# A PDE stage's first slots: four chunks' second parts and the images times 0.3 made ahead of them

## The reference

```
ux, uy = Sobel_x(u), Sobel_y(u)          uxx, uxy, uyy = Sobel of these    (all clipped to +-10)
g2 = ux*ux + uy*uy
K  = clip((uxx*uyy - uxy*uxy) / ((1+g2)^2 + eps), -5, 5)
H  = clip(((1+uy*uy)*uxx - 2*ux*uy*uxy + (1+ux*ux)*uyy) / (2*sqrt(1+g2+eps)^3 + eps), -5, 5)
u  = u + 0.01 * clip(alpha*K + beta*H, -1, 1);   border pixels := their inner neighbours
ten times; result = 0.7*u + 0.3*x
```

## Time and profile before

| | us |
|---|---|
| median of 3 runs | 767.97 (766.85 to 768.89) |
| the profiled execution's own time | 767.58 |
| its span in the profile | 765.8 |
| busy PE / DVE / ACT / POOL | 666.3 / 437.4 / 371.2 / 324.5 |
| curvature stage, from its first stencil product | 424.03 to the end |

### The profile page before, as it was taken

How to read it: one execution, slowest core, us unless ns; L and a number is a source line. 1 busy time by engine, 2 the same in 40 slices (tenths; PEclk the granted TensorE clock), 3 DMA queues, 4 the chain that set the end, 5 groups by cost and what they waited for, 6 DMA issues and landing times.

```text
span 765.8 us, 11096 instructions
## 1 busy us (share of the span) xinstructions
PE 666.3 (87%) x4344; PEld 462.5 (60%) x4344; DVE 437.4 (57%) x642; ACT 371.2 (48%) x620; POOL 324.5 (42%) x311
## 2 busy tenths in 40 slices
PE   5997898999975556688998879999999999999994
PEld 4773774565442223444464768777777878777782
DVE  5630000095041012222434469999999999999997
ACT  1310000060000001110223469999999999999995
POOL 1000000010032400000001469999999999999993
PEclk9999999999995779999999979999999999999997
DMA  9999999999999999999962000000000000000001
GB/s 340 432 406 403 407 419 413 428 421 409 424 401 391 419 427 424 431 427 423 426 274 93 1 0 1 0 0 0 0 0 0 0 0 0 0 0 0 0 0 55
DMA packets 20945, 166.52 MB, mean 217 GB/s; under 512 B 1840, under 2 KB 2224, under 8 KB 11568
## 3 DMA queue, kind: packets, MB, share of 16 engines
q1 hardware_dynamic: 19552, 162.60, 51.5%
q0 software_dynamic: 688, 2.04, 0.8%
q10 hardware_dynamic: 672, 1.41, 0.5%
HBM read 164.99 MB, written 1.05 MB: 217 GB/s over the span
## 4 chain that ended last, share of the span: by engine, by line
DVE 33%; DMA 28%; PE 25%; issue 7%; ACT 4%; POOL 2%; DVEq 0%; POOLq 0%; SPq 0%; ACTq 0%
DMA ring<-wout_w 15%; PE bank L373 6%; DVE ring L863 6%; PE bank L389 5%; DVE ring L868 5%; DVE ring L850 4%; PE bank L523 4%; PE bank L442 4%; PE bank L497 4%; DMA ring<-wv_p 4%; DVE bank L847 3%; DVE bank L883 3%; DMA ring<-wv_w 3%; DMA ring<-wqk_p 3%; DMA ring<-wout_p 3%
## 5 line engine op out<-in xcount | busy, mean ns | idle before, releaser
L574 PE MATMUL bank<-u_parts,vmr 128*128 128x480 f32 x1360 | 313.4, 388 | 13.2 <-DVE ring L863 6.3
L574 PEld LDWEIGHTS bank<-u_parts,vmr 128*128 128x128 f32 x1360 | 253.1, 190 | 73.7 <-DVE reg_a L857 15.4
L389 PE MATMUL bank<-ring,small 128*32 128x256 f32 x1152 | 79.5, 424 | 36.2 <-DMA ring<-wout_w 32.3
L389 PEld LDWEIGHTS bank<-ring,small 128*32 128x32 f32 x1152 | 39.3, 119 | 69.6 <-issue 30.3
L389 PE MATMUL bank<-ring,xw 128*32 128x256 f32 x1024 | 63.9, 410 | 15.8 <-DMA ring<-wv_w 15.8
L1086 POOL MEMSET reg_d<- 128x2176 f32 x1 | 1.9, 1916 | 151.8 <-PE bank L449 151.8
L1114 POOL DMA_DIRECT2D vmr<-vmats x1 | 0.6, 566 | 148.0 <-PE bank L389 148.0
L702 DVE SCALAR_TENSOR_TENSOR reg_a<-bank,prm 128x512 f32<-128x512 f32 x4 | 2.8, 692 | 105.7 <-PE bank L449 105.7
L373 PE MATMUL bank<-reg_a,ring 128*128 128x256 f32 x256 | 57.9, 388 | 3.4 <-DMA ring<-wqk_p 2.6
L389 PEld LDWEIGHTS bank<-ring,xw 128*32 128x32 f32 x1024 | 34.0, 117 | 44.0 <-DMA ring<-wv_w 19.5
L994 ACT ACTIVATE reg_e<-xa 32x384 f32<-32x384 f32 (+7 forms) x20 | 9.1, 457 | 98.3 <-DVE xa L831 72.1
(11 more groups left out here) (195 smaller groups left out, 1008.0 us busy)
## 6 DMA issues: line engine op xcount, KB each, us to landing
ring<-wv_w SPq DMA_DIRECT2D x32, 2048.0 KB, 24.0
ring<-wout_w SPq DMA_DIRECT2D x30, 2048.0 KB, 36.7
ring<-wqk_p SPq DMA_DIRECT2D x4, 2048.0 KB, 20.1
ring<-wqk_w SPq DMA_DIRECT2D x4, 2048.0 KB, 21.9
ring<-wv_p SPq DMA_DIRECT2D x2, 2048.0 KB, 22.9
ring<-wout_p SPq DMA_DIRECT2D x2, 2048.0 KB, 22.5
ring<-wout_w SPq DMA_DIRECT2D x4, 1024.0 KB, 36.0
vmr<-vmats POOLq DMA_DIRECT2D x1, 1664.0 KB, 7.2
```

Of the source, the lines that this page charges most:

```text
L389: ins = te.matmul(bank[32 * j:32 * j + 32, b_, n0:n0 + 256], lhs(c), slot[k % NSLOT][:, c, 256 * j:256 * j + 256], start=start and c == 0, ...
L574: last = te.matmul(dst[:, 0:NF], mat(m, first), p3[:, 2 + off:S + off, :], start=(high and n == 0), stop=(not high and n == len(terms) - 1))
```

## The change

ACT makes the SECOND parts of all four chunks' `u_hi`, then all four `x3`, before its slot 1; POOL makes the SECOND parts of all four `u_lo` before its slot 1. Slots 1 and 2 hold no `high` and no `low` any more, slots 1 to 4 no `x3`. The instructions are the same in kind, number and size; PE's, DVE's and SP's lists are the same as before.

```diff
 ACT
-            def slot_step(k, q, new, old, c, first=False):
+            def slot_step(k, q, new, old, c):
...
                 if c is not None:
-                    high(k + 2, c, not first or k + 2 > NCH)
+                    high(k + 2, c, True)
...
                 a.activation(fields_in(q, 0, 2), den[q].rearrange("p (x n) -> p x n", x=2), ACT.Exp,
                              scale=-1.0).then_inc(ac["inv"], 1)
-                if first and k <= NCH:
-                    a.activation(x3[:, k - 1, :], u_in(k - 1), ACT.Copy, scale=0.3).then_inc(ac["x3"], 1)
...
-            for x in range(2):
+            for x in range(NCH):
                 high(x + 1, x, False)
+            for x in range(NCH):
+                a.activation(x3[:, x, :], u_in(x), ACT.Copy, scale=0.3).then_inc(ac["x3"], 1)
             a.wait_ge(ve["scales"], 1)
             for k in range(1, LOOP_FROM):
-                slot_step(k, k % 2, True, k > 1, (k + 1) % NCH, True)
+                slot_step(k, k % 2, True, k > 1, (k + 1) % NCH if k + 2 > NCH else None)
 POOL
-            def slot_step(k, q, c, new, old, later=True, border=None):
+            def slot_step(k, q, c, new, old, border=None):
...
                 if c is not None:
-                    low(k + 1 if later else k + 2, c, later)
+                    low(k + 1, c)
...
-            for x in range(2):
+            for x in range(NCH):
                 low(x + 1, x, False)
             for k in range(1, LOOP_FROM):
                 if k + 2 <= NCH:
-                    slot_step(k, k % 2, k + 1, True, k > 1, False)
+                    slot_step(k, k % 2, None, True, k > 1)
                 else:
-                    slot_step(k, k % 2, k % NCH if k >= NCH else None, True, True, True, (k - 3) % NCH)
+                    slot_step(k, k % 2, k % NCH if k >= NCH else None, True, True, (k - 3) % NCH)
```

More of the change, by code:

```diff
@@ L1158, in _ @@
                 if k + 2 <= NCH:
-                    slot_step(k, k % 2, k + 1, True, k > 1, False)
+                    slot_step(k, k % 2, None, True, k > 1)
                 else:
-                    slot_step(k, k % 2, k % NCH if k >= NCH else None, True, True, True, (k - 3) % NCH)
+                    slot_step(k, k % 2, k % NCH if k >= NCH else None, True, True, (k - 3) % NCH)
             with p.Fori(1, LOOPS + 1) as i:
                 for m in range(NCH):
-                    slot_step(i * NCH + (m + 3), (m + 3) % 2, (m + 3) % NCH, True, True, True, m % NCH)
+                    slot_step(i * NCH + (m + 3), (m + 3) % 2, (m + 3) % NCH, True, True, m % NCH)
             for k in range(LOOP_END, SLOTS + 2):
-                slot_step(k, k % 2, k % NCH if k < SLOTS else None, k <= SLOTS, True, True, (k - 3) % NCH if k + 2 <= SLOTS else None)
+                slot_step(k, k % 2, k % NCH if k < SLOTS else None, k <= SLOTS, True, (k - 3) % NCH if k + 2 <= SLOTS else None)
     return nc
```

## The result

The changed kernel takes 758.07 us (median of 4 runs, 757.21 to 759.15) against 768.43 for the kernel before (four runs; the 767.97 given ahead is the median of the first three): ratio 0.9869, 95% interval 0.9848 to 0.9889, so 10.4 us faster. The forecast was 757.5, range 755.9 to 761.0. The profiled execution has a span of 756.5 us (765.8 before).

The account below looks back on a forecast made before the run. The prediction took the bound to be one wait handed from ACT's late high through POOL and DVE to PE in slots 1 and 2. Gains of 9.5 + 1.0 = 10.5 us from 767.97 gave 757.5, range 755.9 to 761.0.

Parts of the forecast that it names:

- Part 1: Work put ahead of slot 1 on ACT and POOL: hidden, cost 0, at most 2.7 us.
- Part 2: Slot 1 without low(3): kh(1) at 436.9, 5.0 us earlier, with PE going on without a gap.
- Part 3: Slot 2: kh(2) moves from 454.44 to 444.96, 9.5 us earlier.
- Part 4: Slots 3 to 6: the 1.05 us excess, put down to x3 on ACT, goes; 1.0 us gained, lower bound 0.
- the prediction's own sign of being wrong: Slots 3 to 6: kh(2) to kh(6) over 31.8 us would show the forecast wrong.
- x3 costs only where slots 3 and 4 show an excess: ACT, slots 1 to 4: x3 costs 0.52 us each in slots 3 and 4; slots 1 and 2 did theirs in idle time.
- PE's count of 10.6 us: Check on PE alone: idle 4.06 + 2.26 and slow 2.77 + 1.55 us, against 10.5 on DVE.
- the ring: Steady run of the curvature stage's slots after the stalls, 7.90 us each from kh(6) to kh(39).
- ACT is the engine without slack: Steady slots: ACT taken to have no slack, since two x3, 1.04 us, match the excess of slots 3 and 4.
- The clock didn't fall: Rival at the stage's start: PE's clock falls to 1.2 GHz all the same, 760 to 761.5 us; chance 0.06.
- no other wait took over: Rival in slot 2 or 3: another wait brings one stall back in part, 759.5 to 763 us; chance 0.08.
- the slower rival: Slots 7 to 40 lock into another phase and each pays; at 0.5 us per slot 774.5 us; chance 0.03.

Follow-up runs that it names:

- high_only: Kernel before with all four high put ahead of slot 1, low and x3 left in their slots: 758.65 us against 767.56.
- low_late: Kernel before with POOL's low(3) and low(4) moved behind absum in slots 1 and 2: 761.11 us against 768.06.
- head_plus8: Changed kernel with eight dead 512-column copies added on ACT behind the four x3, ahead of slot 1: 758.49 us.
- head_plus14: Changed kernel with fourteen dead 512-column copies added on ACT ahead of slot 1: 761.11 us.
- x3_only: Kernel before with only the four x3 moved ahead of slot 1, high and low left in place: 767.57 us against 767.56.
- x3_in_slots: Changed kernel with the four x3 put back into slots 1 to 4: 758.64 us against 756.81 for the changed kernel.
- act_short: Changed kernel with ACT's p2 over 16 of its 480 columns in every slot: 758.68 us.
- inv_first: Changed kernel with ACT's inv(k) placed ahead of high(k+2) in every slot: 764.87 us.
- inv_first_short: Changed kernel with inv(k) ahead of high(k+2) and p2 over 16 of 480 columns, both on ACT: 756.19 us.

## Why the prediction was right, step by step

**Part 1, the head: right.** All added work fits in front of slot 1. The slack was estimated at 1.33 us for ACT and 1.2 for POOL, measured 1.22 and 1.20. The upper bound of 2.7 us was too dark: ACT has 4.3 us of cover there, since the first reader is slope(1).

**Part 2, slot 1: right.** kh(1) was to come at 436.9, which is 12.9 behind the first product; it came at 12.94. PE went on without a gap, as said.

**Part 3, slot 2: right in size, 0.2 off.** Forecast 9.5 us for kh(2), measured 30.41 - 20.76 = 9.65. Of these, 9.28 come from high (high_only) and the rest from x3(1), which Part 3 does not name. clipxy(2) came at 438.62, 15.11 behind the first product, against the forecast 15.26. One term was wrong without effect: Part 3 takes 0.32 us off the way to inv for the missing high, but from lnd to inv it is 1.10 us in slot 1 now and was 1.23, so only 0.13 came off. DVE, not inv, was last in slot 2. That the cause is POOL's blocked list, and neither the amount of work in the slots nor that low stands in them, is shown by low_late and high_only.

**Part 4, slots 3 to 6: a quarter too high.** Forecast 1.0 us from kh(2) to kh(6), measured 32.65 - 31.89 = 0.76; the prediction's own sign of being wrong, more than 31.8 us there, was met. Slots 4 and 5 gave back 0.52 and 0.51 as said. Slot 3 took 8.17 us instead of 7.90. In it ACT makes a pause that no other engine ends: line 1042 starts 1.15 us behind 1038, elsewhere 0.87, and inv(3) and kh(3) are late by it. head_plus8 has the same pause six instructions earlier in ACT's list, ahead of line 1054 of slot 2 (0.97 us behind 1051 instead of 0.68), where it holds up nothing, and its slot 3 takes 7.91. head_plus14 has it eleven instructions earlier, at line 1042 of slot 2. So it moves with what stands ahead of it in ACT's list; what it is stays open. The accounting "x3 costs only where slots 3 and 4 show an excess" holds for the kernel before (x3_only, 1.08) but not for the new one, where x3 left in the slots costs 1.53 (x3_in_slots). The idle time that hid the first two was the stall that the change removes.

**The total.** 9.65 + 0.76 makes 10.41, and 10.43 was measured against 10.5. That it is so close is partly luck: Part 3 was 0.15 too low and Part 4 0.24 too high.

**The clock: the fact right, the argument weak.** It stayed at 1.00. But PE's count of 10.6 us was no second proof: idle and slow time of PE and the delays of kh are read from the same stretch and must come out alike. The low clock itself cost nothing in before that a run shows: at full clock and with x3 in place, slots 4 and 5 are as long (8.42, x3_in_slots and low_late) as in before (8.43, 8.41). PE's slow products lay in time in which the ring waited anyway. That doesn't hold everywhere: in head_plus14 they cost 0.2 us of slot 3.

**"ACT is the engine without slack": half true.** It is so for anything put between up_h and inv or behind inv while the list is full; taking work away from one place on ACT gains nothing (act_short).

**Rivals.** The clock didn't fall; no other wait took over, apart from the 0.27 us of slot 3; the period held 7.90 in the changed kernel. That every slot can become longer is real, inv_first shows it with 0.20 us per slot; but there it is the longer list of ACT and not the slower rival's change of phase, which no run shows. The change didn't alter the order inside the loop.

## What to carry to other kernels

Look for a wait whose releaser stands late in its own engine's list while what is queued behind the waiter feeds everyone: here one early-placed 0.8 us instruction left POOL idle for 7 us, DVE for 6 and PE for 4, and mending either end of the wait alone brought most of the gain (8.9 or 7.5 of 10.4 us). Idle time that hides work may be the very stall you are about to remove, so price hidden work anew for the kernel after the change. When several engines tie at the same period, shortening one operation shows nothing; count the loops through them, and test the order of a list as well as its length. An independent instruction between two dependent ones may be hiding their hand-over: taking it out from between them cost 0.2 us per slot.

## What the runs showed of the hardware

A DVE operation of 480 columns with both inputs in SBUF, beside a busy POOL, took 1345 ns against 646 with one input in PSUM, one of 960 columns 1204 against 1145; POOL's operations beside them grew from 1232 to 2144 ns and from 255 to 673 ns for a 32-column one. Together this made 1.00 us per slot (8.83 against inv_first_short's 7.83). On ACT, an instruction of 960 columns was followed by an independent one after 0.91 us, by one that reads its result after 1.10 to 1.11. PE's clock fell to 1.2 GHz after an idle gap of 2.26 us in the profile of the kernel before and after one of 2.12 us in head_plus14 (0.50 from 445 to 447); in x3_only the gap at the same place was 2.70 us, and the clock behind it 1.00. The length of the gap alone doesn't tell which it will be.
